# Causal attention: exps of two key chunks in one instruction, and a shorter list of pending PV products

## The reference

```python
x = x + _layernorm(_L0_attn_ref(_layernorm(x), w_in, w_out))
x = x + _layernorm(_L0_ffn_ref(_layernorm(x), weight, bias, gate_w, ics, ocs))

# attention: 32 query heads, 8 key/value heads, head size 128
scores = jnp.einsum('bqhgd,bkhd->bhgqk', qg, k) * scale
scores = jnp.where(causal[None, None, None, :, :], scores, -1e+30)
probs = jax.nn.softmax(scores, axis=-1)
out = jnp.einsum('bhgqk,bkhd->bqhgd', probs, v)
```

## Time and profile before

| | us |
|---|---|
| median of 2 runs | 10148.99 |
| lowest, highest | 10073.87, 10224.11 |
| profiled execution | 10206.26 |
| span of its slowest core (core 3) | 10204.7 |
| spans of the eight cores | 10083.1 to 10204.7 |
| TensorE busy, share of the span | 6518.1, 64% |
| VectorE busy | 1822.3, 18% |
| ScalarE busy | 1752.0, 17% |

### The profile page before, as it was taken

The page is one execution under the profiler, slowest core; times in us unless marked ns, Lnnn a source line. Parts: engine busy times, 40 slices in busy tenths (PEclk is TensorE's granted clock), DMA queues, the critical chain, the costliest instruction groups (busy, mean ns, idle before and its releaser), DMA issues.

```text
span 10204.7 us, 67201 instructions; the slowest of 8 cores (10083.1 to 10204.7 us)
## 1 busy us (share of the span) xinstructions
PE 6518.1 (64%) x22496; PEld 2204.3 (22%) x22496; DVE 1822.3 (18%) x1540; ACT 1752.0 (17%) x2929; POOL 247.9 (2%) x283
## 2 busy tenths in 40 slices
PE   1377777784667777777777777589871028889500
PEld 1133333331111111111111111233331013333200
DVE  3211111102321111111101000000004452000144
ACT  2100000002332222222222222000002221111111
POOL 0011111100000000000000000000000000000000
PEclk5677888896555555555555555798775558999755
DMA  2211111222000000000000000421212231221233
GB/s 84 71 35 37 38 38 38 39 54 77 10 25 6 6 21 4 4 4 4 3 3 3 3 3 3 112 49 32 47 46 103 115 111 29 48 48 33 75 144 132
DMA packets 118321, 442.99 MB, mean 43 GB/s; under 512 B 13665, under 2 KB 87521, under 8 KB 88033
## 3 DMA queue, kind: packets, MB, share of 16 engines
q0 software_dynamic: 16912, 119.74, 6.4%
q10 hardware_dynamic: 12962, 176.18, 4.4%
q1 hardware_dynamic: 88128, 142.78, 3.8%
HBM read 415.78 MB, written 142.61 MB: 55 GB/s over the span
## 4 chain that ended last, share of the span: by engine, by line
PE 63%; DMA 12%; DVE 11%; ACT 7%; issue 5%; another core or an unknown queue 1%; POOL 1%; ACTq 0%; DVEq 0%; POOLq 0%; SPq 0%
PE PA L544 6%; PE PB L358 5%; PE PA L358 5%; DVE recT_sb L605 4%; DMA wq_sb<-wqkv 4%; PE PB L562 3%; PE PB L572 3%; PE PB L691 3%; PE PA L691 3%; PE PF L537 3%; PE PE L537 3%; PE PB L853 3%; PE PA L853 3%; DVE stats L228 3%; DMA x_t<-xin 3%
## 5 line engine op out<-in xcount | busy, mean ns | idle before, releaser
L605 DVE RECIPROCAL recT_sb<-PA 1x512 f32<-1x512 f32 x128 | 428.3, 3346 | 2595.5 <-PE PA L544 2595.5
L544 PE MATMUL PA<-ptb,ones_bf 128*1 128x512 bf16 (+3 forms) x1280 | 664.3, 519 | 0.0
L358 PE MATMUL PB<-arena,wq_sb 128*128 128x512 bf16 x2048 | 490.4, 404 | 125.0 <-DMA wq_sb<-wqkv 125.0
L358 PE MATMUL PA<-arena,wq_sb 128*128 128x512 bf16 x2048 | 489.1, 404 | 109.7 <-DMA wq_sb<-wqkv 109.7
L608 PE MATMUL PA<-recT_sb,ones_f 1*128 1x512 f32 x256 | 261.3, 1122 | 460.6 <-DVE recT_sb L605 460.6
L537 PE MATMUL PE<-ptb,vtm 128*128 128x512 bf16 (+3 forms) x640 | 342.6, 535 | 235.9 <-ACT ptb L594 235.9
L537 PE MATMUL PF<-ptb,vtm 128*128 128x512 bf16 (+3 forms) x640 | 342.8, 536 | 235.1 <-ACT ptb L594 235.1
L594 ACT ACTIVATE ptb<-PB 128x512 bf16<-128x512 f32 (+1 forms) x640 | 333.5, 573 | 662.2 <-PE PB L572 651.9
L562 PE MATMUL PB<-q_sb,k_sb 128*128 128x512 bf16 (+1 forms) x640 | 371.8, 581 | 1.3
L572 PE MATMUL PB<-nmxT_sb,ones_bf 1*128 1x512 bf16 (+1 forms) x640 | 371.8, 581 | 0.0
L691 PE MATMUL PB<-wslot,arena 128*128 128x512 bf16 x1344 | 333.9, 416 | 57.3 <-DMA wslot<-wout 57.3
(11 more groups left out here) (192 smaller groups left out, 6444.7 us busy)
## 6 DMA issues: line engine op xcount, KB each, us to landing
x_t<-xin ACTq DMA_DIRECT2D x32, 2048.0 KB, 9.3
wq_sb<-wqkv POOLq DMA_DIRECT2D x48, 1024.0 KB, 9.3
wslot<-wout POOLq DMA_DIRECT2D x32, 1024.0 KB, 17.2
x2s<-ln2tmp SPq DMA_DIRECT2D x16, 2048.0 KB, 6.2
wslot<-wffn POOLq DMA_DIRECT2D x32, 1024.0 KB, 16.3
x_t<-x2s ACTq DMA_DIRECT2D x16, 2048.0 KB
out<-y_t SPq DMA_DIRECT2D x16, 2048.0 KB, 9.7
Qs<-qout_sb SPq DMA_DIRECT2D x128, 128.0 KB, 7.3
```

The costliest lines, as they stand in the source:

```text
L358: do("tensor", lambda e, p=p, ec=ec, tb=tb, a=sl["ap"]: e.matmul(a[:, :], wq_sb[p][:, ec * 128:(ec + 1) * 128], arena[:, ec * S + tb * 512 ...
L544: e.matmul(sums_ap[0:1, j0 * 128: j0 * 128 + cw], ones_bf1[:, 0:1], ptb[pb][:, j0 * 128: j0 * 128 + cw], start=(kc == 0), stop=(kc == nkc ...
L605: vrc = do("vector", lambda e, sp=sp: e.reciprocal(recT_sb[sp][0:1, :], sums_ap[0:1, 0:512]), inc="sV", waits=(("sT", pe_grp),))
```

## The change

Three things change, all in attention. First, where both chunks of a pair are off the diagonal, one activation instruction takes the exp of both, 1024 columns from two neighbouring PSUM banks (`PB`, or `PCD`, which joins `PC` and `PD`) into one buffer `ptb2` of twice the width, of which there are three. Pairs on the diagonal keep two instructions. Second, PVs are issued while more than two are pending, not three. Third, `mk_nmx` runs two groups ahead and not three. The diff, cut:

```diff
-    ptb = [al(f"ptb{i}", [128, 512], BF16, offset=S0 + i * 1024) for i in range(6)]
+    ptb2 = [al(f"ptb2_{i}", [128, 1024], BF16, offset=S0 + i * 2048) for i in range(3)]
...
-    PC = nc.alloc_psum_tensor("PC", [128, 512], F32)
-    PD = nc.alloc_psum_tensor("PD", [128, 512], F32)
+    PCD = nc.alloc_psum_tensor("PCD", [128, 1024], F32)
+    PC = PCD[:, 0:512]
+    PD = PCD[:, 512:1024]
...
+    stpair = [PB[:, 0:1024], PCD[:, 0:1024]]
...
+            po = (pb % 2) * 512
...
-                   ptb[pb][:, j0 * 128: j0 * 128 + cw],
+                   ptb2[pb // 2][:, po + j0 * 128: po + j0 * 128 + cw],
...
+            pairable = (len(pair) == 2 and pair[0][2] == 0 and pair[1][2] == 0
+                        and pair[0][0] % 4 in (0, 2) and pair[0][1] + 1 == pair[1][1])
+            if pairable:
+                kci0, pb0 = pair[0][0], pair[0][1]
+                sp2 = stpair[(kci0 % 4) // 2]
+                wex = (("sT", pe_st),)
+                if pbuf_user[pb0]:
+                    wex = wex + (("sT", pbuf_user[pb0]),)
+                if pbuf_user[pb0 + 1]:
+                    wex = wex + (("sT", pbuf_user[pb0 + 1]),)
+                ec_ = do("scalar", lambda e, pb0=pb0, sp2=sp2: e.activation(
+                    ptb2[pb0 // 2][:, :], sp2, AF.Exp, bias=0.0, scale=1.0),
+                    inc="sA", waits=wex)
+                stbank[kci0 % 4]["exp"] = ec_
+                stbank[(kci0 + 1) % 4]["exp"] = ec_
+                pend_pv.append(pair[0])
+                pend_pv.append(pair[1])
+            else:
...
-            while len(pend_pv) > 3:
+            while len(pend_pv) > 2:
                 emit_pv(*pend_pv.pop(0))
...
-            while next_nmx[0] < NG and next_nmx[0] <= g + 3:
+            while next_nmx[0] < NG and next_nmx[0] <= g + 2:
```

More of the change, by code:

```diff
@@ L199, in build_program @@
         dict(ap=PB[:, 512:1024], eng="scalar", pe_done=0, ev_done=0),
-        dict(ap=PC[:, :], eng="vector", pe_done=0, ev_done=0),
-        dict(ap=PD[:, :], eng="scalar", pe_done=0, ev_done=0),
+        dict(ap=PC, eng="vector", pe_done=0, ev_done=0),
+        dict(ap=PD, eng="scalar", pe_done=0, ev_done=0),
     ]
@@ L468, in build_program @@
     stbank = [dict(ap=PB[:, 0:512], exp=0), dict(ap=PB[:, 512:1024], exp=0),
-              dict(ap=PC[:, :], exp=0), dict(ap=PD[:, :], exp=0)]
+              dict(ap=PC, exp=0), dict(ap=PD, exp=0)]
+    stpair = [PB[:, 0:1024], PCD[:, 0:1024]]
     sums_banks = [PA[:, 512:1024], PA[:, 512:1024]]
@@ L535, in emit_pv @@
                 wpv = wpv + (("sV", pvb["free"]), ("sA", max(bc_last)))
-            do("tensor", lambda e, kc=kc, H=H, pb=pb, j0=j0, cw=cw, nkc=nkc,
+            po = (pb % 2) * 512
+            do("tensor", lambda e, kc=kc, H=H, pb=pb, j0=j0, cw=cw, nkc=nkc, po=po,
                a=pvb["ap"]: e.matmul(
@@ L539, in emit_pv @@
                    vtm[:, kc * 1024 + H * 128: kc * 1024 + (H + 1) * 128],
-                   ptb[pb][:, j0 * 128: j0 * 128 + cw],
+                   ptb2[pb // 2][:, po + j0 * 128: po + j0 * 128 + cw],
                    start=(kc == 0), stop=(kc == nkc - 1)),
                inc=None, waits=wpv)
-            do("tensor", lambda e, kc=kc, pb=pb, j0=j0, cw=cw, nkc=nkc:
+            do("tensor", lambda e, kc=kc, pb=pb, j0=j0, cw=cw, nkc=nkc, po=po:
                e.matmul(sums_ap[0:1, j0 * 128: j0 * 128 + cw], ones_bf1[:, 0:1],
-                        ptb[pb][:, j0 * 128: j0 * 128 + cw],
+                        ptb2[pb // 2][:, po + j0 * 128: po + j0 * 128 + cw],
                         start=(kc == 0), stop=(kc == nkc - 1)),
@@ L587, in mk_ph2 @@
             pe_st = cnt("sT")
[L588 to L598, removed]
@@ L599, in mk_ph2 @@
-            while len(pend_pv) > 3:
+            pairable = (len(pair) == 2 and pair[0][2] == 0 and pair[1][2] == 0
[16 more added lines that the diff above has]
+            else:
+                for (kci, pb, j0, cw) in pair:
+                    bk = stbank[kci % 4]
+                    wex = (("sT", pe_st),) if kci == pair[0][0] else ()
+                    if pbuf_user[pb]:
+                        wex = wex + (("sT", pbuf_user[pb]),)
+                    po = (pb % 2) * 512
+                    bk["exp"] = do("scalar", lambda e, pb=pb, j0=j0, cw=cw, po=po,
+                                   a=bk["ap"]:
+                                   e.activation(
+                                       ptb2[pb // 2][:, po + j0 * 128: po + j0 * 128 + cw],
+                                       a[:, j0 * 128: j0 * 128 + cw], AF.Exp,
+                                       bias=0.0, scale=1.0),
+                                   inc="sA", waits=wex)
+                    pend_pv.append((kci, pb, j0, cw))
```

## The result

The changed kernel takes 9631.21 us in the median of 11 runs (9577.32 lowest), the kernel before 10164.31 us (10073.87 lowest) on the same chips. The ratio is 0.9481, with a 95% interval of 0.9438 to 0.9524: 5.2% faster. Between the lowest times of the two the difference is 497 us, between the medians 533. The forecast was 9660 us with a range of 9560 to 9780.

The account below looks back on a forecast made before the run. TensorE was taken to bound attention, its idle time including needless PV waits on exps. Stalls -492, norms -2 and clock +6 gave -488 us; scaling the median by 0.952 gave 9663, subtracting 9661, so 9660 us, range 9560 to 9780.

Parts of the forecast that it names:

- The reading of L533: At the PV's emission it reads its bank's last noted exp, so 384 PVs wait for an exp they don't need.
- the stalls: TensorE's 384 PV waits on an exp in attention all go with the shorter pending list: -492 us.
- the loss of clock: Higher-clock spells after five PVs at group ends might vanish with four: +6 us, bounds 0 and 12.
- the norms: Norm chains two groups ahead: first scores 4.2 us earlier, one late group some 2.0 us more; net -2 us.
- The start-to-start price: Stalls priced from matmul start to start, 1.45, 1.34 or 0.89 us by pair type, summing to 492 us.
- the joined exp: Off-diagonal pairs: 1.02 us per 1024-column exp saves ScalarE some 65 us, covered by TensorE, so worth 0.
- The slack at a group start: First exps of a group end 0.85 us before PV 0, some 0.7 with the signal, so no wait.
- Stalls that stay: Rival: the PV waited for something other than the noted exp; 10150 us, chance 3%.
- a new partial wait: Rival: slow joined exp or lost group-start slack; 9730 us, or 9905 if half the gain is lost; chance 5%.
- the slower case: Rival: the two-bank exp is so slow that each pair loses time; 10350 us, chance 2%.
- The 7.4 us row of before: Trace of unbroken scores, bias rows and a PV granted 0.50 throughout; taken as evidence against a clock rise.
- that rival: The clock rises inside the groups, first 5 us of each left low: about 1010 us saved, 8650 us, chance 6%.

Follow-up runs that it names:

- e3: Kernel before, with each PV waiting for its own exp's number, three still pending; 9654.97 us median, ratio 0.947 to before, attention 3428.7 us.
- e1: Kernel before, with only the pending list cut from three to two; 9689.74 us median, ratio 0.9495 to before, attention 3431.3 us.
- e4: Kernel before, with only the norms run two groups ahead instead of three; attention 3915.2 us, ratio 0.996 to before.
- e2: Changed kernel with pending list and norm lead set back to three, leaving the joined exp alone; ratio 0.9972 to before, attention 3917.4 us.
- e5: Changed kernel with the bias matmul given 128 rows, 127 of them zero; 8630.87 us median, ratio 0.855 to before, attention 2474.9 us.
- e6: Kernel before, stalls kept, with the bias matmul given 128 rows; 9422.94 us median, ratio 0.916 to before, attention 3027.0 us.

## Why the prediction was right

*What bounds the kernel* held: TensorE's order, with idle time in one place. The reading of L533 was right, and e3 shows it with nothing else changed.

*The sum.* Predicted for the stage -492 - 2 + 6 = -488 us; measured -488.8. That it met the measured value to 1 us is in part luck: the stalls were taken 3.2 us too high and the loss of clock 3.4 us too high, and the two cancel. By parts: the stalls with the lost clock spells -486.2 (e1; -492 + 6 = -486 was worked out), what e1 lacks against e3, taken for the spells, +2.6 (6 was taken, bounds 0 and 12), so the stalls themselves 488.8 (492), the norms -2.3 (-2), the joined exp -0.1 (0). The start-to-start price stood 21 us above the idle figure of 471; the measured 488.8 stands 18 above it, so the runs are on that side. The bound of 498 in the prediction's range is worked out nowhere; nothing hung on it.

*The joined exp* took 1.023 us, as the extrapolation from 128 and 512 columns gave. It hid behind TensorE as said. The slack at a group start was there: joined exp from 5606.02 to 5607.04, PV 0 at 5607.90 with no wait in the changed kernel.

*The whole program.* The ratio worked out was 0.952, the measured 0.9481, its interval reaching to 0.9524. Attention accounts for 489 of the 533 us between the medians. The rest, some 44 us, is no part of the change that a trace shows; between the lowest times, 497 us, hardly any is left. The two profiled executions differ by 618 us of span, some 130 more than attention gives. The prediction had named a move of other stages by over 70 us as a sign of being wrong, so this needs an answer. It is not the change: outside attention the profiled execution of before took 2468.2 us ahead (median of the cores) and 3779.5 behind, against 2425.5 and 3709.7 in the changed kernel, but 2427.3 and 3710.6 in e4 and 2427.2 and 3712.1 in e2, which have the stalls too. So the execution on which the sum was made spent about 110 us more than these in stages that the change doesn't touch, more than the 57 us by which it stood above its median. Taking the sum in us from the median (9661) was as close as one could be with this.

*The rivals.* Stalls that stay, a new partial wait and the slower case did not come. The clock stayed at 0.50 in 28.6 us of unbroken work. The 7.4 us row of before was the right witness against it. But the size of that rival was about right: once the one-row matmuls were gone, attention fell by 954 us, where 1010 were worked out. That its 8650 stands within 20 us of e5's 8630.87 is partly chance: e5 also gained from the shorter steps, which the rival did not count, and its groups of tb = 0 gained nothing. The 5 us that it left low in each group came from no row; e5 shows some 4. The rule of the Trainium skill, "TensorE: Matmul & The Clock Gate", Part 1 (What's actually happening), that sustained activity releases the clock, agrees with e5 and not with the changed kernel, if activity is read as TensorE having no gap; the runs show that this reading is not enough.

## What to carry to other kernels

A wait taken from a table of "the last user of this buffer" is only right when it is read before the next user is noted; keep the number with the item that waits. When an engine waits for one that is mostly idle, ask which instruction of it is waited for before making that engine faster: the joined exp gained nothing that can be told (0.1 us), the right number 489 us. And look at the clock granted in a busy stretch before counting its matmuls: the 128-row edit, with the shorter steps that came with it, was worth 954 us here, twice the change.

## What the runs showed of the hardware

- TensorE kept to 1.2 GHz through 28.6 us without a gap while two of eight matmuls fed a single row; with 128 rows, 127 of them zero, it was granted 2.4 GHz after about 4 us of each longer group: attention 3428.7 to 2474.9 us. The same edit shortened the steps, and the two were not separated.
- At the lower level a score matmul of 512 columns next to a one-row matmul steps by 0.54 us, next to a 128-row matmul with 128 weight columns by 0.43. The difference is about one weight load (0.10 us).
- Waits of 1.4 us in each pair did not bring the upper level down (e6: granted clock 1.00 from 5000 to 5013 us with three of them).
- An exp of 1024 columns over two PSUM banks takes 1.023 us, two of 512 take 1.08 us together; in the pairs shown it starts 0.05 us later, so that the gain on a waiting engine is 0.02 us.
